# Decoder layer, feed-forward stage: tiles 8 to 15's reciprocals are split in three pieces by GpSimd instead of VectorE, and turned behind tile 7's first product

## The chip, the cores and the metric

The kernel runs on one core of a Trainium2 chip. The metric is the device time of one execution in microseconds (us); lower is better. Engines are called by their names: TensorE (PE in the profile, PEld for its weight loads), VectorE (DVE), ScalarE (ACT), GpSimd (POOL) and SyncE (SP), which issues the DMAs.

## What is computed

One post-norm decoder layer over 8 x 256 tokens of 512 numbers: self-attention with 16 heads, cross-attention, and a feed-forward part; after each the input is added and the sum normalised. Only the feed-forward part is touched. From the reference, cut:

```
def activation_quant(x):
    scale = 127.0 / jnp.clip(jnp.max(jnp.abs(x), axis=-1, keepdims=True), EPS, None)
    return jnp.clip(jnp.round(x * scale), -128.0, 127.0) / scale
def bitlinear(x, w, b):
    return jnp.einsum('bsd,fd->bsf', activation_quant(x), weight_quant(w)) + b
h = bitlinear(x, w1, b1)                # 512 -> 2048
h = jax.nn.gelu(h, approximate=False)
h = layernorm(h, gamma, beta)
return bitlinear(h, w2, b2)             # 2048 -> 512
```

weight_quant makes each weight -1, 0 or 1 times one factor. Each token row has a scale of its own in each of the two products.

## The kernel before

The 2048 tokens are 16 tiles of 128 rows, tile t = 0 to 15 (TILES). The feed-forward stage is a software pipeline over t in which each engine has a program of its own; engines meet only at semaphores, and each runs its own instructions in the order written. In round t of its loop (line numbers are those of the kernel before):

- TensorE: first product of tile t, `up(t, f)` for f = 0 to 3, each four matmuls with the weights (L1846) and one with the bias (L1847) into one of four PSUM banks; then the second product of tile t - 3, `down(t-3)`, one matmul L1864 and sixteen L1869. `up` waits for the gelu of the tile before to have emptied the banks, two banks at a time. Since the products are made with whole numbers, the bias must be divided by the row's factor: the reciprocal of that factor, split in three bf16 pieces (high, middle, low), stands as six rows for each token in `recips`, and L1847 multiplies them, turned into `rT`, with `bias_rows`.
- ScalarE: `gelu(t, 0)` and `gelu(t, 1)` (L2074, two banks each), `norm_y(t-4)` (L2115), `square(t)` (L2083), `round_h(t-1)` (L2094, to bytes), `spread_y(t-3)` (L2106, L2109).
- VectorE: `mean(t)` (L1969, one small instruction), `scale_gamma(t)` (L1979), `take_y(t-3)` (L2016), `norm_h(t)` (L1988), `scale_h(t)` (L1994, L1999, L2004).
- GpSimd: `bias_acc(t-2)` (L2154), `root_h(t)` (L2159, and L2164, a power), `round_x(t+3)` and `cut_x(t+3)` (L1932, L1939), `scale_out(t-1)` (L2169), `centre_y(t-3)` (L2180, a power L2185, and L2189).
- SyncE: turns `xq` into `xT` and `hq` into `hT` by DMA (L1793, L1803 to L1808) and stores the output.

What waits for what in a tile: `mean(t)` waits for both halves of gelu(t), square(t) for mean(t), root_h(t) for square(t), norm_h(t) for root_h(t), round_h(t) for scale_h(t), down(t) for the turned round_h(t), norm_y(t) for centre_y(t).

The reciprocals are made for eight tiles at a time. `scales(dve, 1)` (L1903 to L1927) does tiles 8 to 15 on VectorE in round 5 between take_y(2) and norm_h(5): nine instructions on 128x8 numbers. The first four make the scale of x (L1910, which round_x(8) on GpSimd waits for) and the reciprocal itself (L1913); the last five split it in three pieces. In round 7 TensorE turns the pieces for all eight tiles (`turn_recips`, two groups of four transposes, L1951) and ScalarE copies them from PSUM (`take_recips`, two copies L1956). The first product of tile 8 waits for the first of these copies, in this line of `up`:

```
if f == 0 and t % 4 == 0:
    pe.wait_ge(s["rT_ready"], t // 4 + 1)
```

Each copy waits for all eight transposes.

Of the kernel before, what the change touches and what calls it, by code (L numbers as in the profile page):

```python
# [12 lines left out]
ALU = mybir.AluOpType  # L13
# [3 lines left out]
P = 128  # L17
# [1682 lines left out]
def feed_forward(nc, T, out, env, keep):  # L1700
# [11 lines left out]
    with ExitStack() as ctx:  # L1712
# [3 lines left out]
        def sb(name, shape, dt=F32):  # L1716
# [29 lines left out]
        xg, xsc, xd, xr, hd, gsum, nm, ss, ve, rstd, hmax, hg, hs, ystats, ymv, yv, yr, ym, m_half, shift, ysum, ynm, yss = (  # L1746
            small[:, at:at + n] for at, n in zip(
                places, (16, 16, 16, 48, 16, 4, 2, 2, 2, 2, 2, 2, 2, 12, 4, 2, 2, 2, 1, 1, 2, 2, 2)))
        one = ones[:].bitcast(BF16)[:, 1:2]
        xr = xr.rearrange("p (c t) -> p c t", c=3)  # L1750
# [6 lines left out]
        s = {n: sem("f_" + n) for n in names}  # L1757
# [9 lines left out]
        def live(t):  # L1767
            return 0 <= t < TILES
# [63 lines left out]
        def tensor(pe):  # L1832
            def up(t, f):
                if f == 0:
                    pe.wait_ge(xT_in[t % 3], (t // 3 + 1) * 16)
                    if t == 0:
                        pe.wait_ge(w_in[0], 16)
                if f == 0 and t % 4 == 0:
                    pe.wait_ge(s["rT_ready"], t // 4 + 1)
                if t == 0:  # L1840
                    pe.wait_ge(env["shared_sems"]["rows_in"], 3 * 16)
                if f % 2 == 0 and t > 0:
                    pe.wait_ge(s["gelu_ready"], (t - 1) * 2 + f // 2 + 1)
                cols = slice(f * 512, (f + 1) * 512)
                for c in range(CH):
                    pe.matmul(psH[f], turned_x(t)[:, c, :], w1[:, c, cols], start=c == 0, stop=False)  # L1846
                pe.matmul(psH[f], rT[:, t, :], bias_rows[:, cols], start=False, stop=True).then_inc(s["f1"], 1)  # L1847

            def sum_w2():
                pe.wait_ge(w_in[1], 16)  # L1850
                pe.wait_ge(s["rT_ready"], 2)
                for k in range(FCH):
                    last = pe.matmul(psR[0:1, :], one, w2[:, k, :], start=k == 0, stop=k == FCH - 1)
                last.then_inc(s["w2_summed"], 1)

            def down(t):
                if t == 0:
                    pe.wait_ge(s["sums_ready"], 1)
                    pe.wait_ge(s["fconsts"], 33)
                if t > 1:  # L1860
                    pe.wait_ge(s["y_ready"], t - 1)
                else:
                    pe.wait_ge(env["shared_sems"]["y_out"], TILES - 1 + t)
                pe.matmul(psO[t % 2], less_base[:], w2_sums[:], start=True, stop=False)  # L1864
                pe.wait_ge(hT_in[t % 2], (t // 2 + 1) * 16)
                for k in range(FCH):
                    if t == TILES - 1 and k == HALF:
                        pe.wait_ge(last_in, 16)
                    last = pe.matmul(psO[t % 2], hT[:, t % 2, k, :], w2[:, k, :], start=False, stop=k == FCH - 1)  # L1869
                last.then_inc(s["f2"], 1)  # L1870

            tail = env["tail"]
            pe.wait_ge(env["shared_sems"]["clipped"], TILES * 4)
            for t in range(TILES + 3):
                if t == 7:
                    turn_recips(pe, 2)
                    turn_recips(pe, 3)
                for f in range(4):
                    if live(t):
                        up(t, f)  # L1880
                if t == 0:
                    tail["mix"]()
                if t == 1:
                    sum_w2()
                if t == 2:
                    tail["output"](0)
                    tail["output"](1)
                if live(t - 3):
                    down(t - 3)
# [13 lines left out]
        def scales(dve, g):  # L1903
            lo, hi = PARTS[g]
            now, n = slice(lo, hi), hi - lo
            dve.wait_ge(env["x_maxed"], hi)
            nc.vector.tensor_scalar(xg[:, now], xmax[:, now], EPS, 1.0 / QMAX, ALU.max, ALU.mult
                                    ).then_inc(s["x_guarded"], 1)
            dve.wait_ge(s["x_guarded"], 2 * g + 1)
            nc.vector.reciprocal(xsc[:, now], xg[:, now]).then_inc(s["x_scaled"], 1)  # L1910
            nc.vector.tensor_scalar(xd[:, now], xg[:, now], w_mean[:, 0:1], None, ALU.mult).then_inc(s["x_guarded"], 1)
            dve.wait_ge(s["x_guarded"], 2 * g + 2)
            nc.vector.reciprocal(xr[:, 0, now], xd[:, now]).then_inc(s["r_set"], 1)  # L1913
            dve.wait_ge(s["r_set"], 3 * g + 1)
            nc.vector.tensor_copy(recips[:, now, 0:3], xr[:, 0, now].unsqueeze(2).broadcast_to([P, n, 3])
                                  ).then_inc(s["r_split"], 1)
            dve.wait_ge(s["r_split"], 3 * g + 1)
            nc.vector.tensor_tensor(xr[:, 1, now], xr[:, 0, now], recips[:, now, 0], ALU.subtract
                                    ).then_inc(s["r_set"], 1)
            dve.wait_ge(s["r_set"], 3 * g + 2)  # L1920
            nc.vector.tensor_copy(recips[:, now, 3:5], xr[:, 1, now].unsqueeze(2).broadcast_to([P, n, 2])
                                  ).then_inc(s["r_split"], 1)
            dve.wait_ge(s["r_split"], 3 * g + 2)
            nc.vector.tensor_tensor(xr[:, 2, now], xr[:, 1, now], recips[:, now, 3], ALU.subtract
                                    ).then_inc(s["r_set"], 1)
            dve.wait_ge(s["r_set"], 3 * g + 3)
            nc.vector.tensor_copy(recips[:, now, 5], xr[:, 2, now]).then_inc(s["r_split"], 1)  # L1927

        def round_x(pool, t):
            if t in (lo for lo, _ in PARTS):  # L1930
# [23 lines left out]
        def take_recips(act, j):  # L1954
            act.wait_ge(s["r_turned"], j // 2 * 2 + 2)
            nc.scalar.copy(rT[:, 4 * j:4 * j + 4, :].rearrange("p t n -> p (t n)"),  # L1956
                           psR[:, (j % 2) * 256:(j % 2 + 1) * 256].bitcast(BF16)[0:6, :]
                           ).then_inc(s["rT_ready"], 1)
# [109 lines left out]
        def scalar(act):  # L2068
# [50 lines left out]
            for t in range(TILES + 4):  # L2119
                if live(t):  # L2120
                    gelu(t, 0)
                    gelu(t, 1)
                if t == 1:
                    tail["scale_y"](B - 2)
                    tail["late_norm"](B - 3)
                if t == 3:
                    tail["scale_y"](B - 1)
                    tail["late_norm"](B - 2)
                if t == 5:
                    tail["late_norm"](B - 1)  # L2130
                if t == 7:
                    take_recips(act, 2)
                    take_recips(act, 3)
                if live(t - 4) and t - 4 < TILES - 1:
                    norm_y(t - 4)
                if live(t):
                    square(t)
                if t == 0:
                    tail["round_o"]()
                if t == 2:  # L2140
                    take_sums()
                if live(t - 1):
                    round_h(t - 1)
                if live(t - 3) and t - 3 < TILES - 1:
                    spread_y(t - 3)

        def gpsimd(pool):
# [45 lines left out]
            for t in range(0, TILES + 3):  # L2193
                if live(t - 2):
                    bias_acc(t - 2)
                if live(t):
                    root_h(t)
                if t + 3 >= AHEAD and live(t + 3):
                    round_x(pool, t + 3)
                    cut_x(pool, t + 3)  # L2200
                if t == 0:
                    tail["split_o"]()
                    tail["root_sum"](B - 3)
                if t == 1:
                    pool.wait_ge(s["hn_ready"], 2)
                    tail["finish_ahead"](B - 2, 0)
                    tail["finish_ahead"](B - 2, 1)
                if t == 2:
                    tail["root_y"]()
                    tail["root_sum"](B - 2)  # L2210
                if t == 3:
                    pool.wait_ge(s["hn_ready"], 4)
                    tail["finish_ahead"](B - 1, 0)
                if t == 4:
                    tail["root_sum"](B - 1)
                if live(t - 1):
                    scale_out(t - 1)
                if live(t - 3):
                    centre_y(t - 3)
# [81 lines left out]
```

## Time and profile before

| | us |
|---|---|
| median of 3 runs | 1409.6 (1407.73 to 1410.35) |
| the profiled execution, its own time | 1409.61 |
| its span in the profile | 1407.8 |
| TensorE busy | 1373.2 (98%) |
| VectorE busy | 1180.7 (84%) |
| ScalarE busy | 798.8 (57%) |
| GpSimd busy | 646.4 (46%) |

Busy time is summed over all stages; the feed-forward stage takes about the last 170 us of the span. Times in the rows are microseconds from the span's start. In a timeline row the first number is the start, the second the duration; then come the engine, the line and the operation, and in brackets, where there is one, the idle time of the engine ahead of it and what ended it. The span is 1.8 us shorter than the execution's own time.

### The profile page before, as it was taken

The numbers are of one execution on the slowest core, as the hardware profiler recorded it, in microseconds if no ns is written. First come the engines' busy times: TensorE is split into PE (matmuls) and PEld (weight loads), VectorE is DVE, ScalarE is ACT, GpSimd is POOL, SyncE is SP. The second block draws the span as 40 slices with busy tenths as digits, with TensorE's granted clock in tenths as the row PEclk, the third lists the DMA queues.
The fourth block names the chain that finished last, engine by engine and source line by source line (L and its number), as shares of the span: only waits on it lengthen the run. The fifth ranks groups of instructions, "written<-read, shape, count | busy, mean of one in ns | idle before, by whom it ended". The sixth has DMA issues, their size and how long they took to land.

```text
span 1407.8 us, 25519 instructions
## 1 busy us (share of the span) xinstructions
PE 1373.2 (98%) x8642; PEld 1088.5 (77%) x8642; DVE 1180.7 (84%) x1966; ACT 798.8 (57%) x1856; POOL 646.4 (46%) x747
## 2 busy tenths in 40 slices
PE   8999999999999999999999999999999999898997
PEld 6888888888888888888888888887777777642332
DVE  6888888888879888888887888865778889899996
ACT  6444544545445454555555556754556555678895
POOL 6544435235333433433533444561344455656763
PEclk9999999999999999999999999999999999999998
DMA  7301101011010110102112111411000000522454
GB/s 284 121 11 37 62 14 45 30 46 35 28 58 15 45 60 1 31 28 71 53 46 76 60 38 48 147 46 46 17 16 16 16 15 13 193 69 53 101 106 104
DMA packets 73464, 81.00 MB, mean 58 GB/s; under 512 B 45960, under 2 KB 46472, under 8 KB 72846
## 3 DMA queue, kind: packets, MB, share of 16 engines
q1 hardware_dynamic: 73358, 79.78, 18.8%
q8 instruction: 43, 0.70, 0.2%
q14 instruction: 63, 0.52, 0.1%
HBM read 60.88 MB, written 8.40 MB: 49 GB/s over the span
## 4 chain that ended last, share of the span: by engine, by line
PE 79%; issue 7%; DVE 6%; POOL 5%; ACT 1%; DMA 1%; SPq 0%; POOLq 0%; DVEq 0%; ACTq 0%
PE psum L360 16%; PE psum L362 16%; PE psum L361 16%; PE psum L1111 4%; PE psum L425 4%; PE psum L404 4%; PE psum L1112 3%; PE psum L1113 3%; PE psum L413 3%; PE psum L1205 2%; PE psum L427 2%; PE psum L402 2%; PE psum L1217 1%; DVE xinv L1314 1%; PE psum L1222 1%
## 5 line engine op out<-in xcount | busy, mean ns | idle before, releaser
L866 POOL TENSOR_TENSOR qk<-rope_a,rope_b 128x512 f32<-128x512 f32 x128 | 177.1, 1383 | 496.1 <-DVE rope_b L591 496.1
L360 PE MATMUL psum<-x_hi,w_hi 128*128 128x512 f32 x512 | 209.9, 410 | 1.9 <-DVE x_lo L532 1.9
L362 PE MATMUL psum<-x_hi,w_lo 128*128 128x512 f32 x512 | 201.5, 394 | 0.0
L361 PE MATMUL psum<-x_lo,w_hi 128*128 128x512 f32 x512 | 200.7, 392 | 0.0
L591 DVE SCALAR_TENSOR_TENSOR rope_b<-psum,qk_bias,sin 64x512 f32<-64x512 f32 x256 | 191.9, 750 | 3.8
L715 ACT ACTIVATE e<-s 128x384 f32<-128x384 f32 x128 | 66.4, 518 | 208.1 <-DVE s L572 208.1
L360 PE MATMUL psum<-w_hi,x_hi 128*128 128x256 f32 x512 | 147.5, 288 | 1.2 <-DVE v L614 1.2
L362 PE MATMUL psum<-w_hi,x_lo 128*128 128x256 f32 x512 | 144.8, 283 | 0.0
L361 PE MATMUL psum<-w_lo,x_hi 128*128 128x256 f32 x512 | 144.7, 283 | 0.0
L729 ACT ACTIVATE e<-p 128x128 f32<-128x128 f32 x128 | 39.3, 307 | 175.8 <-DVE p L600 175.8
L634 DVE TENSOR_TENSOR acc<-psum,acc 128x512 f32<-128x512 f32 x128 | 88.5, 692 | 59.8 <-PE psum L362 44.0
L873 POOL TENSOR_TENSOR p<-p,inv 128x128 f32<-128x128 f32 (+1 forms) x256 | 121.7, 506 | 13.6 <-DVE inv L608 13.6
L600 DVE TENSOR_TENSOR p<-e,sgn 128x384 f32<-128x384 f32 x128 | 120.3, 979 | 1.8 <-ACT e L722 0.8
L1540 ACT ACTIVATE xe<-xe,mask_now 128x1024 f32<-128x1024 f32 x64 | 78.8, 1238 | 67.2 <-DVE xe L1307 67.2
L591 DVE SCALAR_TENSOR_TENSOR rope_a<-psum,qk_bias,cos 128x512 f32<-128x512 f32 x128 | 95.3, 744 | 24.8 <-PE psum L362 24.7
L362 PEld LDWEIGHTS psum<-x_hi,w_lo 128*128 128x128 f32 x512 | 96.8, 189 | 21.8
L360 PEld LDWEIGHTS psum<-x_hi,w_hi 128*128 128x128 f32 x512 | 97.2, 190 | 19.6 <-DVE w_lo L528 1.4
L361 PEld LDWEIGHTS psum<-x_lo,w_hi 128*128 128x128 f32 x512 | 97.2, 190 | 17.6
L360 PE MATMUL psum<-w_hi,z_hi 128*128 128x512 f32 x256 | 106.0, 414 | 0.0
L572 DVE SCALAR_TENSOR_TENSOR s<-psum,tri 128x384 f32<-128x384 f32 x128 | 70.7, 552 | 41.6 <-PE psum L404 41.6
L362 PE MATMUL psum<-w_hi,z_lo 128*128 128x512 f32 x256 | 100.4, 392 | 0.0
L361 PE MATMUL psum<-w_lo,z_hi 128*128 128x512 f32 x256 | 100.1, 391 | 0.0
(209 smaller groups left out, 3736.2 us busy)
## 6 DMA issues: line engine op xcount, KB each, us to landing
stage<-w_self_dram SPq DMA_DIRECT2D x64, 256.0 KB, 2.9
w_raw<-w_ffn_dram SPq DMA_DIRECT2D x32, 512.0 KB, 3.6
acc<-x_dram SPq DMA_DIRECT2D x4, 1024.0 KB, 6.0
w_signs<-w_sign SPq DMA_DIRECT2D x16, 256.0 KB, 2.1
xw_raw<-w_cross_dram SPq DMA_DIRECT2D x4, 1024.0 KB, 5.7
c_raw<-ctxT_dram SPq DMA_DIRECT2D x8, 512.0 KB, 3.5
w<-w_signs SPq DMA_DIRECT2D x2, 2048.0 KB, 12.1
out_dram<-yb SPq DMA_DIRECT2D x16, 256.0 KB, 2.3
```

Source lines behind the costliest of these rows:

```text
L360: pe.matmul(ps, ah, bh, start=n == 0, stop=False)
L361: pe.matmul(ps, ah, bl, start=False, stop=False)
L362: last = pe.matmul(ps, al, bh, start=False, stop=n == len(pairs) - 1)
L404: pe.matmul(psS[b][:, P:LW], q[:, b * S + P:(b + 1) * S], kk[:, b * S:(b + 1) * S], start=True, stop=True).then_inc(scores, 1)
L572: nc.vector.scalar_tensor_tensor(s[:, b, :], psS[b][:, 0:LW], SELF_SCALE, tri[:], ALU.mult, ALU.mult).then_inc(s_ready, 1)
L591: last = nc.vector.scalar_tensor_tensor(dst[o, which, :].rearrange("p (b s) -> p b s", b=2), ps[i, :].rearrange("p (b s) -> p b s", b=2), ...
L600: nc.vector.tensor_tensor(p[:, b, :], e[:, b, :], sgn[:, b, :], ALU.mult).then_inc(p_ready, 1)
L634: nc.vector.tensor_tensor(tile, o_bank(n + j)[:, :], tile, ALU.add).then_inc(o_added, 1)
L715: nc.scalar.activation(e[:, b, :], s[:, b, :], ACT.Abs)
L866: nc.gpsimd.tensor_tensor(qk[:, k % 2, which, :], rope_a[:, which, :], rope_b[:, which, :], ALU.add).then_inc(qk_ready, 1)
L873: last = nc.gpsimd.tensor_tensor(p[:, b, cols], p[:, b, cols], inv[:, b, rows:rows + 1].broadcast_to([P, n]), ALU.mult)
L1540: nc.scalar.activation(part, part, ACT.Exp, scale=mask_now[:, par, kt, 0:1], bias=mask_now[:, par, kt, 1:2]).then_inc(e_ready, 1)
```

## The change

Three places move. Of `scales`, the last five instructions become `split_recips`; for tiles 0 to 7 VectorE still runs them where it did, for tiles 8 to 15 GpSimd runs them in its round 5, behind cut_x(8) and ahead of scale_out(4). On TensorE the two turns of round 7 stand behind up(7) instead of ahead of it. On ScalarE the two copies of round 7 stand behind round_h(6) instead of ahead of norm_y(3).

```
@@ tensor
             for t in range(TILES + 3):
+                for f in range(4):
+                    if live(t):
+                        up(t, f)
                 if t == 7:
                     turn_recips(pe, 2)
                     turn_recips(pe, 3)
-                for f in range(4):
-                    if live(t):
-                        up(t, f)
@@ scales
             nc.vector.reciprocal(xr[:, 0, now], xd[:, now]).then_inc(s["r_set"], 1)
-            dve.wait_ge(s["r_set"], 3 * g + 1)
-            nc.vector.tensor_copy(recips[:, now, 0:3], xr[:, 0, now].unsqueeze(2).broadcast_to([P, n, 3])
-                                  ).then_inc(s["r_split"], 1)
...
-            dve.wait_ge(s["r_set"], 3 * g + 3)
-            nc.vector.tensor_copy(recips[:, now, 5], xr[:, 2, now]).then_inc(s["r_split"], 1)
+            if g == 0:
+                split_recips(dve, nc.vector, g)
+
+        def split_recips(eng, ops, g):
+            lo, hi = PARTS[g]
+            now, n = slice(lo, hi), hi - lo
+            eng.wait_ge(s["r_set"], 3 * g + 1)
+            ops.tensor_copy(recips[:, now, 0:3], xr[:, 0, now].unsqueeze(2).broadcast_to([P, n, 3])
+                            ).then_inc(s["r_split"], 1)
+            eng.wait_ge(s["r_split"], 3 * g + 1)
+            ops.tensor_tensor(xr[:, 1, now], xr[:, 0, now], recips[:, now, 0], ALU.subtract
+                              ).then_inc(s["r_set"], 1)
...
@@ scalar
-                if t == 7:
-                    take_recips(act, 2)
-                    take_recips(act, 3)
                 if live(t - 4) and t - 4 < TILES - 1:
                     norm_y(t - 4)
                 if live(t):
                     square(t)
...
                 if live(t - 1):
                     round_h(t - 1)
+                if t == 7:
+                    take_recips(act, 2)
+                    take_recips(act, 3)
                 if live(t - 3) and t - 3 < TILES - 1:
                     spread_y(t - 3)
@@ gpsimd
+                if t == 5:
+                    split_recips(pool, nc.gpsimd, 1)
                 if live(t - 1):
                     scale_out(t - 1)
```

What stands in a row on ScalarE in round 7, from gelu(7) to gelu(8), with the semaphores that an instruction waits for in brackets. Before:

```order
L2074 ACTIVATE h,fsmall<-psum,fsmall 128x1024 [waits f_u_ready,f_f1] x2
L1956 COPY rT<-psum 6x512 [waits f_r_turned] x2
L2115 ACTIVATE yb<-yb,fsmall 128x512 [waits f_y_centred]
L2083 ACTIVATE fspare,fsmall<-h,fsmall 128x2048 [waits f_vared,f_mean_ready]
L2094 ACTIVATE hq<-hn,fsmall 128x2048 [waits hT_in_0,f_h_scaled]
L2106 ACTIVATE fsmall<-fsmall 128x1 [waits f_y_centred,f_y_ready]
L2109 ACTIVATE fspare,fsmall<-yb,fsmall 128x512 [waits f_y_spread]
L2074 ACTIVATE h,fsmall<-psum,fsmall 128x1024 [waits f_u_ready,f_f1] x2
```

The same place on ScalarE in the changed kernel (its lines are numbered six higher):

```order
L2080 ACTIVATE h,fsmall<-psum,fsmall 128x1024 [waits f_u_ready,f_f1] x2
L2121 ACTIVATE yb<-yb,fsmall 128x512 [waits f_y_centred]
L2089 ACTIVATE fspare,fsmall<-h,fsmall 128x2048 [waits f_vared,f_mean_ready]
L2100 ACTIVATE hq<-hn,fsmall 128x2048 [waits hT_in_0,f_h_scaled]
L1962 COPY rT<-psum 6x512 [waits f_r_turned] x2
L2112 ACTIVATE fsmall<-fsmall 128x1 [waits f_y_centred,f_y_ready]
L2115 ACTIVATE fspare,fsmall<-yb,fsmall 128x512 [waits f_y_spread]
L2080 ACTIVATE h,fsmall<-psum,fsmall 128x1024 [waits f_u_ready,f_f1] x2
```

The two copies of `rT` moved back past norm_y(3), square(7) and round_h(6).

GpSimd in round 5 of the changed kernel, from root_h(5) to root_h(6); fsmall holds all the small per-row numbers:

```order
L2170 TENSOR_TENSOR fsmall<-fsmall 128x1 [waits f_hn_ready,f_vared]
L1938 TENSOR_SCALAR xs<-acc,fsmall 128x512 [waits f_x_scaled]
L1945 TENSOR_SCALAR xq<-xs 128x512 [waits xT_in_0,f_xs_ready]
L1921 CAST recips<-fsmall 128x8x3 [waits f_r_set]
L1924 TENSOR_TENSOR fsmall<-fsmall,recips 128x8 [waits f_r_split]
L1927 CAST recips<-fsmall 128x8x2 [waits f_r_set]
L1930 TENSOR_TENSOR fsmall<-fsmall,recips 128x8 [waits f_r_split]
L1933 CAST recips<-fsmall 128x8 [waits f_r_set]
L2175 TENSOR_TENSOR fsmall<-fsmall,w_mean 128x1 [waits f_h_guarded]
L2186 TENSOR_SCALAR fsmall<-fsmall 128x1 [waits f_y_spread]
L2191 TENSOR_TENSOR fsmall<-fsmall 128x1 [waits f_y_normed,f_y_guarded]
L2195 TENSOR_SCALAR fsmall<-fsmall 128x1 [waits f_y_rooted]
```

The five rows from L1921 to L1933 are new there; before, scale_out(4) (now L2175) followed cut_x(8) (now L1945) directly.

VectorE in round 5, the end of `scales` and what follows it, before:

```order
L1913 RECIPROCAL fsmall<-fsmall 128x8 [waits f_x_guarded]
L1915 CAST recips<-fsmall 128x8x3 [waits f_r_set]
L1918 TENSOR_TENSOR fsmall<-fsmall,recips 128x8 [waits f_r_split]
L1921 CAST recips<-fsmall 128x8x2 [waits f_r_set]
L1924 TENSOR_TENSOR fsmall<-fsmall,recips 128x8 [waits f_r_split]
L1927 CAST recips<-fsmall 128x8 [waits f_r_set]
L1988 SCALAR_TENSOR_TENSOR hn<-hn,fsmall,beta 128x2048 [waits f_u_ready,f_rooted]
```

In the changed kernel norm_h(5) follows L1913 directly.

## Rows read from the trace of the kernel before

**Rows 1.** Busy time by engine, granted clock (PEclk), from 1286 to 1394 us.

```profile
1286.00:1394.00 108.00, 99.28 (x406) 35.09 (x405) 104.77 (x114) 96.21 (x138) 68.91 (x104) 0.95 0.46 99
```

**Rows 2.** Timeline of VectorE, rounds 5 to 8 and tile 15's mean.

```profile
1298.63 0.20 DVE L1913 RECIPROCAL fsmall<-fsmall 128x8 f32<-128x8 f32 x1
...
1300.38 2.35 DVE L1988 SCALAR_TENSOR_TENSOR hn<-hn,fsmall,beta 128x2048 f32<-128x2048 f32 x1
...
1308.67 2.79 DVE L1988 SCALAR_TENSOR_TENSOR hn<-hn,fsmall,beta 128x2048 f32<-128x2048 f32 x1
...
1322.88 0.21 DVE L1969 TENSOR_SCALAR fsmall<-fsmall 128x1 f32<-128x1 f32 x1
1323.13 2.42 DVE L1979 SCALAR_TENSOR_TENSOR hn<-h,fsmall,gamma 128x2048 f32<-128x2048 f32 x1
...
1326.26 2.79 DVE L1988 SCALAR_TENSOR_TENSOR hn<-hn,fsmall,beta 128x2048 f32<-128x2048 f32 x1
...
1383.50 0.21 DVE L1969 TENSOR_SCALAR fsmall<-fsmall 128x1 f32<-128x1 f32 x1
```

**Rows 3.** Timeline of GpSimd, rounds 5 and 6.

```profile
1298.61 0.69 POOL L1932 TENSOR_SCALAR xs<-acc,fsmall 128x512 f32<-128x512 f32 x1 [1.32 <-DVE fsmall L1910]
...
1300.54 2.60 POOL L2185 TENSOR_TENSOR fsmall<-fsmall 128x1 f32<-128x1 f32 x1
...
1308.63 0.69 POOL L1932 TENSOR_SCALAR xs<-acc,fsmall 128x512 f32<-128x512 f32 x1
1309.40 2.53 POOL L1939 TENSOR_SCALAR xq<-xs 128x512 bf16<-128x512 f32 x1
...
1312.45 0.55 POOL L2185 TENSOR_TENSOR fsmall<-fsmall 128x1 f32<-128x1 f32 x1
1313.12 0.26 POOL L2189 TENSOR_SCALAR fsmall<-fsmall 128x1 f32<-128x1 f32 x1
```

**Rows 4.** Timeline of ScalarE, rounds 6 to 8.

```profile
1303.55 0.81 ACT L2115 ACTIVATE yb<-yb,fsmall 128x512 f32<-128x512 f32 x1 [2.07 <-POOL fsmall L2189]
1305.60 2.00 ACT L2083 ACTIVATE fspare<-h,fsmall 128x2048 f32<-128x2048 f32 x1 [1.24 <-DVE fsmall L1969]
...
1312.71 1.03 ACT L1956 COPY rT<-psum 6x512 bf16<-6x512 bf16 x2
...
1316.35 2.08 ACT L2094 ACTIVATE hq<-hn,fsmall 128x2048 uint8<-128x2048 f32 x1
...
1320.36 1.10 ACT L2074 ACTIVATE h<-psum,fsmall 128x1024 f32<-128x1024 f32 x1
```

**Rows 5.** Timeline of TensorE, rounds 5, 6, 8 and 9.

```profile
1278.05 1.02 PE L1846 MATMUL psum<-w,xT_ahead 128*128 128x512 bf16 x4 [2.07 <-ACT h L2074]
...
1290.51 1.27 PE L1846 MATMUL psum<-w,xT_ahead 128*128 128x512 bf16 x4 [3.48 <-ACT h L2074]
...
1298.41 0.38 PE L1847 MATMUL psum<-bias_rows,rT 6*128 6x512 bf16 x1
...
1313.37 1.02 PE L1846 MATMUL psum<-w,xT 128*128 128x512 bf16 x4 [1.33 <-ACT rT L1956]
...
1318.18 0.39 PE L1847 MATMUL psum<-bias_rows,rT 6*128 6x512 bf16 x1
...
1322.18 1.03 PE L1846 MATMUL psum<-w,xT 128*128 128x512 bf16 x4
```

**Rows 6.** Busy time and granted clock (0.50) inside the product at 1290.51.

```profile
1292.00:1294.00 2.00, 2.00 (x5) 0.43 (x4) 1.90 (x5) 1.97 (x4) 1.88 (x3) 0.50 0.71 138
```

**Rows 7.** Timeline of TensorE, the second products of tiles 14 and 15.

```profile
1392.19 5.97 PE L1869 MATMUL psum<-w,hT 128*128 128x512 bf16 x16 [3.91 <-DMA hT<-hq]
...
1398.41 3.63 PE L1869 MATMUL psum<-w,hT 128*128 128x512 bf16 x16
```

**Rows 8.** Timeline of SyncE's queue, issue of tile 15's first half.

```profile
1393.18 1.23 SPq L1805 DMA_TRANSPOSE hT<-hq  x1
```

**Rows 9.** The tile hT: its 17 transposing DMAs, from issue to landing.

```profile
DMA to landing us min/median/max: 3.1/4.3/4.9
```

More of the change, by code:

```diff
@@ L1913, in scales @@
             nc.vector.reciprocal(xr[:, 0, now], xd[:, now]).then_inc(s["r_set"], 1)
-            dve.wait_ge(s["r_set"], 3 * g + 1)
-            nc.vector.tensor_copy(recips[:, now, 0:3], xr[:, 0, now].unsqueeze(2).broadcast_to([P, n, 3])
-                                  ).then_inc(s["r_split"], 1)
[L1917 to L1925, printed above, removed]
-            dve.wait_ge(s["r_set"], 3 * g + 3)
-            nc.vector.tensor_copy(recips[:, now, 5], xr[:, 2, now]).then_inc(s["r_split"], 1)
+            if g == 0:
[9 more added lines that the diff above has]
+                              ).then_inc(s["r_set"], 1)
+            eng.wait_ge(s["r_set"], 3 * g + 2)
+            ops.tensor_copy(recips[:, now, 3:5], xr[:, 1, now].unsqueeze(2).broadcast_to([P, n, 2])
+                            ).then_inc(s["r_split"], 1)
+            eng.wait_ge(s["r_split"], 3 * g + 2)
+            ops.tensor_tensor(xr[:, 2, now], xr[:, 1, now], recips[:, now, 3], ALU.subtract
+                              ).then_inc(s["r_set"], 1)
+            eng.wait_ge(s["r_set"], 3 * g + 3)
+            ops.tensor_copy(recips[:, now, 5], xr[:, 2, now]).then_inc(s["r_split"], 1)
         def round_x(pool, t):
```

## The prediction

> **What bounds the kernel now.** I read the busy time of the stage first, then the timeline of each engine around the edit. From 1286 to 1394 us VectorE is busy 104.8 of 108 us [rows 1], so a reader's first thought is that work taken off it is time saved. But TensorE stands beside it as a second bound: from tile 8's first product to tile 9's it takes 8.81 us (1313.37 to 1322.18) [rows 5], and VectorE takes 8.80 us a tile (norm_h(6) at 1308.67, norm_h(8) at 1326.26, two tiles in 17.59) [rows 2]. What keeps the two apart is slack, not speed: up(8) ended at 1318.57 (1318.18 + 0.39) [rows 5], and mean(8), which needs its last gelu, ran at 1322.88 [rows 2]. From the end of a product to the mean behind it at least 1.27 us pass: a start of 0.04, the second gelu 1.10 with the read of its sum, about 1.19 together, and 0.04 [rows 4]. So TensorE is 1322.88 - 1318.57 - 1.27 = 3.04 us early at tile 8. What makes it later than that is paid, and since it can't run faster than 8.81 us a tile, it isn't won back.
>
> **Part one, the five instructions leave VectorE.** L1913 starts at 1298.63 and norm_h(5) at 1300.38 [rows 2]. Without the split norm_h(5) follows L1913 by some 0.08, at 1298.71, 1.67 us earlier. There it meets round_x(8) on GpSimd, 1298.61 to 1299.30 [rows 3]. One round later the same pair meets the same way: GpSimd's xs at 1308.63 for 0.69 (to 1309.32), norm_h(6) at 1308.67, which took 2.79 instead of 2.35 and ended at 1311.46, 2.14 behind xs's end [rows 2, 3]. So norm_h(5) ends at 1299.30 + 2.14 = 1301.44 instead of 1302.73: VectorE gains 1.29. mean(6) comes 2.63 behind norm_h's end (8.80 a tile, less 3.38 from mean to norm_h, less 2.79), at 1304.07, and scale_gamma(6) 0.25 later, at 1304.32 [rows 2].
>
> **Part two, the five instructions on GpSimd.** cut_x(8) now runs into norm_h(5), as cut_x(9) did into norm_h(6): from 1309.40 it took 2.53, to 1311.93, 0.47 behind norm_h's end [rows 2, 3]. So GpSimd comes to the split at 1301.44 + 0.47 = 1301.91. The trace has no such instruction on GpSimd. Nearest are its one-number operations: scale_out and the next one take 0.52 together (1311.93 to 1312.45) [rows 3], 0.26 each. These are 8 to 24 numbers wide, and each waits for the one before; I take 0.28, 1.40 us in all. The low end is VectorE's pace of 0.20 for such instructions, 1.0; the high end 0.69 each, what GpSimd takes for 512 numbers [rows 3], 3.4.
>
> Then come scale_out(4) and the start of centre_y(2), 0.52, its power at 1303.83, and 0.67 later (1312.45 to 1313.12) [rows 3] its multiply L2189, at 1304.50. That is 0.18 behind scale_gamma(6). And a small GpSimd instruction that starts while VectorE works on two inputs in SBUF is held to its end: the power at 1300.54 took 2.60 beside norm_h(5), against 0.55 at 1312.45 [rows 3]; it ended at 1303.14, 0.41 behind norm_h's 1302.73. scale_gamma(6) itself is held by the power (to 1304.38) and ends about 2.14 later, 1306.52; the multiply ends 0.13 behind it (0.41 less the 0.28 by which it is shorter), 1306.65.
>
> The Trainium skill speaks against the edit here (Perfetto Trace Analysis, Optimizing Scalar/DVE Operations: since GpSimd and VectorE share a read port of SBUF, moving work between those two might not help), and says which of them waits (SBUF — State Buffer, Who interferes with whom: whoever starts first keeps the port for the whole instruction). By that rule all hangs on 0.18 us of issue order; were the port shared in bandwidth, the multiply would end near 1304.8 and the sum would be that of the second rival below.
>
> norm_y(2) waits for this multiply already now (ScalarE idle 2.07, start 1303.55), and square(6) stands behind it in ScalarE's program [rows 4]. norm_y(2) now starts at 1306.68 and square(6) 0.8 later, 1307.5, instead of 1305.60: 1.9 late. norm_h(6) follows square(6) by 3.07 as before (1305.60 to 1308.67) [rows 2, 4], and round_h(6) is at 1316.35 + 1.9 = 1318.25 [rows 4]. VectorE's gain is gone.
>
> **Part three, the turn and the copies.** On TensorE the eight transposes swap places with up(7); they take the same in either place, the split is done by 1303.3, and down(4) ends where it did: 1313.37 - 1.33 = 1312.04 [rows 5]. up(8) waited 1.33 us for the first copy of rT, which started at 1312.71; product and copy are 0.66 apart [rows 4, 5]. Now the copies stand behind square(7) and round_h(6). round_h(6) takes 2.08 with 0.09 of overlap, so they start at 1318.25 + 1.99 = 1320.24, and up(8) at 1320.90: 7.5 us late, after 8.9 us of idle TensorE. What waits on ScalarE behind the copies, spread_y(4) and gelu(8), waits for up(8) anyway. Their old place gives nothing back: they ended at 1313.74 (1312.71 + 1.03) [rows 4], and square(7) had to wait for mean(7) at 1314.08 (1322.88 less 8.80) with only norm_y(3) between.
>
> **The clock.** up(6) started at 1290.51 after 3.48 us idle and ended at 1298.79, 8.28 us, where up(8) took 5.20 [rows 5]; inside it the granted clock was 0.50, the 1.2 GHz level [rows 6]. After 2.07 us idle four matmuls took 1.02, full speed [rows 5]. 8.9 us is past the longer of these, so I give up(8) 8.28 us: end 1329.18. The Trainium skill (TensorE: Matmul & The Clock Gate, The HAM clock gate) says that the engine returns to half clock when idle and that the number of slow matmuls at the start differs from run to run.
>
> **The sum.** mean(8) is at 1329.18 + 1.27 = 1330.45, 7.6 late. VectorE reaches mean(9) at 1339.25. TensorE starts up(9) 3.61 behind the end of up(8) as before (1318.57 to 1322.18) [rows 5], at 1332.79, and ends at 1337.99, which allows mean(9) at 1339.26: both engines now set the pace and TensorE is the slower. mean(15) = 1339.26 + 6 x 8.81 = 1392.1 instead of 1383.50 [rows 2]: 8.6 late. The end gives some of it back. Before, down(14) waited 3.91 us for its turned tile and then took 5.97 us at low clock, so down(15) started only at 1398.41, 3.63 long [rows 7], though its first half was issued at 1393.18 [rows 8] and landed 3.1 later [rows 9], at 1396.3. Now TensorE is 10.6 late (1322.18 to 1332.79) and the tile 8.6, so the wait is 3.91 - 2.0 = 1.9 us, under the 2.07 that left the clock up: down(14) takes 3.6 and down(15) starts when its half lands, 1396.3 + 8.6 = 1404.9, 6.5 later than before. After it nothing changes. 1409.61 + 6.5 = **1416.1**; the profiled execution stands at the median of 1409.6, so that needs no correction.
>
> **The rivals.**
> - *The long way* (0.21). The split takes over 1.9 us, the power itself meets scale_gamma(6) and waits too: 0.7 more, 1416.8. Or the clock falls before down(14) as well: 2.3 us more, 1418.4. Against the latter: 1.9 against 2.07.
> - *GpSimd slips through* (0.17). If the split takes under 1.2 us, the multiply starts ahead of scale_gamma(6), square(6) isn't late (about 0.2 early), and 2.1 us fall away: 1414.0. For it: only 0.18 us decide.
> - *The clock holds in up(8)* (0.10). 3.1 less: 1413.0. Against it: 0.50 after a shorter idle.
> - *The saving reaches the end* (0.05), not slower: VectorE's 1.29 us are carried through all later tiles, 1408.3. It decides at TensorE's slack of 3.04: up(8) would have to start before 1313.37 + 3.04 - 1.29 = 1315.1 at full clock. Against it: the copies can't start ahead of round_h(6)'s end, 1318.4 without any other delay; moving that up by all of 1.29 gives up(8) at 1317.7.
> - *Both small mercies* (0.03), GpSimd through and the clock up: 1409.61 + 6.5 - 2.1 - 3.1 = 1410.9, no change.
>
> **The numbers.** The forecast has 0.44. Within 0.2% (2.8 us, about what a measurement of this kernel can tell) lie the last two rivals, 0.08 less a little; faster needs more than VectorE can save at all, 0.01; slower 0.91. The range 1412.0 to 1419.0 leaves out the last two rivals, and of the long way the case in which both of its delays come together (1409.61 + 6.5 + 0.7 + 2.3 = 1419.1) or a third joins them; between them about 0.13.
>
> **What the profile after would show.** norm_h(5) at 1298.7 for about 2.8; five GpSimd instructions from 1301.9 for 1.4; centre_y(2)'s multiply held to about 1306.6; square(6) near 1307.5; TensorE idle some 9 us with the copy as its releaser, up(8) near 1320.9, 8.3 long at clock 0.5; mean(8) near 1330.4 with VectorE idle ahead of it; down(14) at full clock. Wrong would be: rT ready early, or TensorE running tiles in under 8.81 us once it is the late one, which would win the loss back.

## The result, and the profile after

| | us |
|---|---|
| before, median of 5 runs in the same job | 1409.57 (1407.73 to 1410.35) |
| changed kernel, median of 5 runs | 1417.14 (1415.96 to 1418.31) |
| ratio | 1.0056, 95% interval 1.0046 to 1.0067 |
| its profiled execution: own time, span | 1418.24, 1416.4 |

The change makes the kernel 7.6 us slower. The forecast was 1416.1 with a range of 1412.0 to 1419.0. The rows that answer to those of before follow; lines of the changed kernel are numbered six higher from L1915 on (norm_h is L1994, mean L1975, scale_gamma L1985). All times of this execution lie 1.29 us later than those of before already at L1913 (1299.92 against 1298.63 [rows 2]); where that comes from is told at the end, and the comparisons below are made from L1913 on.

Timeline of VectorE: start, duration, instruction, idle ahead and what ended it.

```profile
1299.92 0.20 DVE L1913 RECIPROCAL fsmall<-fsmall 128x8 f32<-128x8 f32 x1
1300.04 2.68 DVE L1994 SCALAR_TENSOR_TENSOR hn<-hn,fsmall,beta 128x2048 f32<-128x2048 f32 x1
...
1305.60 2.35 DVE L1985 SCALAR_TENSOR_TENSOR hn<-h,fsmall,gamma 128x2048 f32<-128x2048 f32 x1
...
1311.86 2.79 DVE L1994 SCALAR_TENSOR_TENSOR hn<-hn,fsmall,beta 128x2048 f32<-128x2048 f32 x1 [3.24 <-POOL fsmall L2170]
...
1331.62 0.21 DVE L1975 TENSOR_SCALAR fsmall<-fsmall 128x1 f32<-128x1 f32 x1 [5.47 <-ACT h L2080]
...
1340.63 0.21 DVE L1975 TENSOR_SCALAR fsmall<-fsmall 128x1 f32<-128x1 f32 x1
...
1393.36 0.21 DVE L1975 TENSOR_SCALAR fsmall<-fsmall 128x1 f32<-128x1 f32 x1 [0.16 <-ACT h L2080]
```

VectorE had no wait here before. Now it has two long ones: 3.24 us ahead of norm_h(6), and 5.47 us ahead of mean(8). What it saved shows in the first two rows: norm_h(5) 0.12 behind L1913 instead of 1.75.

Timeline of GpSimd, round 5 and the power of root_h(6).

```profile
1300.67 2.53 POOL L1945 TENSOR_SCALAR xq<-xs 128x512 bf16<-128x512 f32 x1
1303.15 0.21 POOL L1921 CAST recips<-fsmall 128x24 bf16<-128x24 f32 x1
...
1304.29 0.21 POOL L1933 CAST recips<-fsmall 128x8 bf16<-128x8 f32 x1
...
1304.99 0.55 POOL L2191 TENSOR_TENSOR fsmall<-fsmall 128x1 f32<-128x1 f32 x1
1305.66 2.42 POOL L2195 TENSOR_SCALAR fsmall<-fsmall 128x1 f32<-128x1 f32 x1
...
1311.28 0.55 POOL L2170 TENSOR_TENSOR fsmall<-fsmall 128x1 f32<-128x1 f32 x1
```

The five instructions take 0.21 each and follow each other by some 0.28, and nothing holds them. The multiply L2195 starts at 1305.66, 0.06 behind scale_gamma(6) at 1305.60, and takes 2.42 instead of 0.26 [rows 3]: it is held until scale_gamma(6) has ended (1307.95), and ends 0.13 behind it.

Timeline of ScalarE: norm_y(2), square(6), round_h(6), the two copies.

```profile
1308.11 0.81 ACT L2121 ACTIVATE yb<-yb,fsmall 128x512 f32<-128x512 f32 x1 [5.35 <-POOL fsmall L2195]
1308.84 1.99 ACT L2089 ACTIVATE fspare<-h,fsmall 128x2048 f32<-128x2048 f32 x1
...
1319.53 2.08 ACT L2100 ACTIVATE hq<-hn,fsmall 128x2048 uint8<-128x2048 f32 x1
1321.51 1.04 ACT L1962 COPY rT<-psum 6x512 bf16<-6x512 bf16 x2
```

Timeline of TensorE: up(8) from its first to its last matmul, up(9), down(14), down(15).

```profile
1322.17 1.87 PE L1846 MATMUL psum<-w,xT 128*128 128x512 bf16 x4 [9.69 <-ACT rT L1962]
...
1329.96 0.38 PE L1847 MATMUL psum<-bias_rows,rT 6*128 6x512 bf16 x1
...
1333.96 1.03 PE L1846 MATMUL psum<-w,xT 128*128 128x512 bf16 x4
...
1402.35 3.63 PE L1869 MATMUL psum<-w,hT 128*128 128x512 bf16 x16 [2.29 <-DMA hT<-hq]
...
1407.07 3.63 PE L1869 MATMUL psum<-w,hT 128*128 128x512 bf16 x15 [0.78 <-DMA hT<-hq]
```

Busy time and granted clock inside up(8).

```profile
1324.00:1326.00 2.00, 2.00 (x6) 0.49 (x5) 1.93 (x3) 0.00 (x0) 1.72 (x5) 0.50 0.32 66
```

TensorE waits 9.69 us for the first copy (1.33 before [rows 5]), and up(8) then takes 8.17 us, 1322.17 to 1330.34, for the most part at a granted clock of 0.50, the 1.2 GHz level (the last four of its weight matmuls take 1.04 again, full speed). At the end down(14) waits 2.29 us instead of 3.91, and takes 3.63 instead of 5.97 [rows 7].

### The profile page after: what moved, and what is told of

The parts are those of the page before. It is cut to its first block, busy times and chain, and to the rows that moved or that the text cites. A ratio compares the mean times of both kernels' runs of the same rounds, so it can differ in the third digit from the quotient of the medians.

```text
span 1416.4 us, 25505 instructions
## 1 busy us (share of the span) xinstructions
PE 1373.0 (97%) x8628; PEld 1088.6 (77%) x8642; DVE 1180.5 (83%) x1961; ACT 798.7 (56%) x1856; POOL 649.5 (46%) x752
## 4 chain that ended last, share of the span: by engine, by line
PE 79%; issue 7%; DVE 6%; POOL 6%; ACT 1%; DMA 1%; SPq 0%; POOLq 0%; DVEq 0%; ACTq 0%
PE psum L360 16%; PE psum L362 16%; PE psum L361 16%; PE psum L1111 4%; PE psum L425 4%; PE psum L404 4%; PE psum L1112 3%; PE psum L1113 3%; PE psum L413 3%; PE psum L1205 2%; PE psum L427 2%; PE psum L402 2%; PE psum L1217 2%; PE psum L1222 1%; DVE xinv L1314 1%
```

## The experiments

Eight kernels. Each took its ratio against the kernel before, run beside it on the same chip; x1 to x4 ran in one job (before 1409.42, 29 runs), x5 to x8 in another (before 1409.16, 23 runs). The last column is from the one profiled execution of each: the time from L1913 to the end of the span, less the 109.17 us (1407.8 - 1298.63) of before. The changed kernel has +7.3 there.

| kernel | median, us | ratio | 95% interval | from L1913 on, us |
|---|---|---|---|---|
| x1_turn_copies | 1414.32 | 1.0036 | 1.0023 to 1.0049 | +8.8 |
| x2_copies_early | 1412.84 | 1.0020 | 1.0011 to 1.0029 | +1.0 |
| x3_split_behind | 1409.62 | 1.0001 | 0.9993 to 1.0010 | +0.4 |
| x4_square_first | 1410.46 | 1.0007 | 0.9998 to 1.0015 | -0.5 |
| x5_filler | 1413.34 | 1.0033 | 1.0020 to 1.0046 | +5.1 |
| x6_no_split | 1407.47 | 0.9994 | 0.9986 to 1.0003 | -1.8 |
| x7_copies_mid | 1412.86 | 1.0032 | 1.0020 to 1.0044 | +4.0 |
| x8_fill_tail | 1407.17 | 0.9989 | 0.9981 to 0.9998 | -2.0 |

The two measures needn't agree. A single execution carries whatever TensorE's clock did in it, and the ratio carries what lies ahead of the edit too: in these executions L1913 stands anywhere from 1295.56 to 1302.13. So each cause below is read from the trace, as a distance from L1913, and the ratio says only whether it shows in the time.

### x1_turn_copies: the turn and the copies alone

```
-            if g == 0:
-                split_recips(dve, nc.vector, g)
+            split_recips(dve, nc.vector, g)
...
-                if t == 5:
-                    split_recips(pool, nc.gpsimd, 1)
```

> The split stays on VectorE as in the kernel before; only the turn (behind up(7)) and the two copies (behind round_h(6)) are moved. Theory (the late copies starve TensorE): up(8) starts 5.6 us late against the other engines, after some 7 us of idle TensorE, takes 8.2 us at half clock, mean(15) is 6.6 us late, and the time is 4.5 to 5.3 us above before, 1414 to 1415. Rival (the loss comes from GpSimd's held multiply): within 0.5 us of before, 1409.6.

Measured 1.0036, 5.1 us of 1409.4. Timeline of TensorE, up(8):

```profile
1318.43 1.86 PE L1846 MATMUL psum<-w,xT 128*128 128x512 bf16 x4 [8.82 <-ACT rT L1961]
```

L1913 stands at 1298.09 in this execution, so up(8) starts 20.34 behind it, against 14.74 before (1298.63 to 1313.37 [rows 2, 5]): 5.6 late, as the theory has it. By the ratios this half of the change costs about two thirds of the loss, and it has nothing on the other side: no work is saved by it.

Two parts of the expectation missed in this execution. up(8) took 9.46 us, not 8.2, and the low clock went on through down(5):

```profile
1328.25 6.02 PE L1869 MATMUL psum<-w,hT 128*128 128x512 bf16 x16
```

So mean(15) is 10.5 us late, not 6.6. The execution took 1417.89, the slowest of five with a median of 1414.32, so how late mean(15) is in the median run isn't known.

### x2_copies_early: the split on GpSimd alone

The changed kernel with the two copies back ahead of norm_y(3):

```
+                if t == 7:
+                    take_recips(act, 2)
+                    take_recips(act, 3)
                 if live(t - 4) and t - 4 < TILES - 1:
                     norm_y(t - 4)
```

> As the changed kernel, split on GpSimd and turn behind up(7), but the copies of rT in their old place ahead of norm_y(3). Theory: the multiply of centre_y(2) is held, norm_h(6) is 1.9 us late, up(8) waits about as before (1.3 us) and runs at full clock: 1.9 us above before, 1411.5. Rival (without the late copies VectorE's saving reaches the end): 1408.3.

Measured 1.0020, 2.8 us (1.6 to 4.1). With x1 the ratios add up to the whole change, 0.0036 + 0.0020 = 0.0056, which with these intervals is good to about 2 us; the last column doesn't add up (8.8 and 1.0 against 7.3), mostly for x1's clock. Timeline of GpSimd, the multiply:

```profile
1307.84 2.37 POOL L2195 TENSOR_SCALAR fsmall<-fsmall 128x1 f32<-128x1 f32 x1
```

Timeline of VectorE: L1913, norm_h(6), mean(8).

```profile
1302.13 0.20 DVE L1913 RECIPROCAL fsmall<-fsmall 128x8 f32<-128x8 f32 x1
...
1313.99 2.79 DVE L1994 SCALAR_TENSOR_TENSOR hn<-hn,fsmall,beta 128x2048 f32<-128x2048 f32 x1 [3.16 <-POOL fsmall L2170]
...
1328.19 0.21 DVE L1975 TENSOR_SCALAR fsmall<-fsmall 128x1 f32<-128x1 f32 x1
```

Timeline of TensorE, up(8):

```profile
1318.71 1.87 PE L1846 MATMUL psum<-w,xT 128*128 128x512 bf16 x4 [3.19 <-ACT rT L1962]
```

norm_h(6) comes 11.86 behind L1913, 1.82 later than before (10.04). One part of the expectation was wrong: up(8) doesn't wait 1.3 us at full clock but 3.19, and starts at half clock (four matmuls in 1.87). The copies are late with square(6) while TensorE isn't, which the expectation left out. up(8) takes 6.76 us. mean(8) nevertheless stands 26.06 behind L1913, 1.81 more than before (24.25), no more than norm_h(6): TensorE's slack of 3.04 took the rest. At the end 1.0 us is left, since down(14) took 5.08 instead of 5.97.

### x3_split_behind: the same split, four instructions later

```
-                if t == 5:
-                    split_recips(pool, nc.gpsimd, 1)
                 if live(t - 1):
                     scale_out(t - 1)
                 if live(t - 3):
                     centre_y(t - 3)
+                if t == 5:
+                    split_recips(pool, nc.gpsimd, 1)
```

> As x2_copies_early, but GpSimd does the split behind centre_y(2), at the end of its round 5. Theory (what costs is that centre_y(2), which norm_y(2) and square(6) wait for, stands behind the split): the multiply takes 0.26 and ends near 1303.4, square(6) starts 1.2 us earlier than before, the fifth instruction of the split is held by scale_gamma(6) instead, root_h(6) follows late, norm_h(6) 0.2 us later than before: 1409.8. Rival (the split costs 1.4 us on GpSimd wherever it stands): 1411.5.

Measured 1.0001. Timeline of GpSimd: the multiply, the split's fifth instruction.

```profile
1301.66 0.27 POOL L2195 TENSOR_SCALAR fsmall<-fsmall 128x1 f32<-128x1 f32 x1
...
1303.01 2.29 POOL L1933 CAST recips<-fsmall 128x8 bf16<-128x8 f32 x1
```

Timeline of VectorE: L1913, norm_h(6).

```profile
1297.20 0.20 DVE L1913 RECIPROCAL fsmall<-fsmall 128x8 f32<-128x8 f32 x1
...
1307.45 2.79 DVE L1994 SCALAR_TENSOR_TENSOR hn<-hn,fsmall,beta 128x2048 f32<-128x2048 f32 x1 [1.55 <-POOL fsmall L2170]
```

Now the fifth instruction is held, 2.29 for 0.21, and bias_acc(4) and root_h(6) behind it. norm_h(6) is 10.25 behind L1913, 0.21 more than before, where 0.2 was expected. The five instructions cost GpSimd the same time as in x2_copies_early, so it isn't their length alone that costs 1.8 us but who stands behind them. The turn stands behind up(7) here as in the changed kernel, so its place costs nothing that this run shows; what x1_turn_copies pays for is the copies.

### x4_square_first: ScalarE doesn't wait for the multiply

```
-                if live(t - 4) and t - 4 < TILES - 1:
+                if live(t - 4) and t - 4 < TILES - 1 and t != 6:
                     norm_y(t - 4)
                 if live(t):
                     square(t)
+                if t == 6:
+                    norm_y(t - 4)
```

> As x2_copies_early, but ScalarE does square(6) ahead of norm_y(2) in round 6, so that square(6) doesn't wait for GpSimd's multiply. Theory: the multiply is still held to the end of scale_gamma(6), square(6) starts right behind mean(6), 1.3 us earlier than before, but bias_acc(4) and root_h(6) stand behind the multiply on GpSimd, so that norm_h(6) comes out some 0.1 us later than before: 1409.7. Rival (the chain through ScalarE isn't what carries the 1.9 us): the same time as x2_copies_early.

Measured 1.0007 (0.9998 to 1.0015), which includes 1, no change; its median is below x2_copies_early's, though the two intervals overlap. Timelines of GpSimd and VectorE: the held multiply, norm_h(6).

```profile
1307.18 2.42 POOL L2197 TENSOR_SCALAR fsmall<-fsmall 128x1 f32<-128x1 f32 x1
...
1311.78 2.79 DVE L1994 SCALAR_TENSOR_TENSOR hn<-hn,fsmall,beta 128x2048 f32<-128x2048 f32 x1 [1.64 <-POOL fsmall L2172]
```

L1913 stood at 1301.44, so norm_h(6) is 10.34 behind it, 0.30 over before (0.1 was expected) instead of 1.82. The multiply is held as in x2; that it no longer stands ahead of square(6) takes 1.5 us away. That shows the way of the loss: GpSimd's multiply, norm_y(2), square(6).

### x5_filler: TensorE kept busy while it waits

```
+        FILL = 40
...
                 if live(t - 3):
                     down(t - 3)
+                if t == 7:
+                    for k in range(FILL):
+                        pe.matmul(bank[4], xT_ahead[:, 0, k % CH, :], w1[:, k % CH, 0:512], start=k == 0, stop=k == FILL - 1)
```

> The changed kernel, with 40 matmuls of 512 columns on TensorE between down(4) and up(8), into a PSUM bank that nobody reads, so that TensorE isn't idle while it waits for the copies of rT. They take 8.6 us and end about 1 us before the first copy. Theory (the idle time costs a second time, through the clock): up(8) starts as late as in the changed kernel but takes 5.2 us instead of 8.2, mean(8) and all behind it are 3 us earlier, 1414 if the changed kernel is at 1417. Rival (the clock doesn't carry any of the loss, or the fillers delay up(8)): the changed kernel's time or more.

Measured 1.0033 against the changed kernel's 1.0056 (in another job, each by its own runs of before): 3.2 us less, give or take some 2.4. Timeline of TensorE: the fillers, first and last matmul of up(8).

```profile
1310.54 8.80 PE L1893 MATMUL psum<-w,xT_ahead 128*128 128x512 bf16 x39
1320.33 1.02 PE L1847 MATMUL psum<-w,xT 128*128 128x512 bf16 x4 [0.99 <-issue]
...
1325.15 0.39 PE L1848 MATMUL psum<-bias_rows,rT 6*128 6x512 bf16 x1
```

up(8) starts 22.17 behind L1913 (1298.16), as late as in the changed kernel (22.25), and takes 5.21 us instead of 8.17: the clock was worth 3.0 us there, and mean(15) is 3.05 earlier. At the end 2.2 of it is left (5.1 against 7.3 in the last column), because down(14) met the low clock in this execution:

```profile
1397.50 5.31 PE L1870 MATMUL psum<-w,hT 128*128 128x512 bf16 x16 [2.26 <-DMA hT<-hq]
```

### x6_no_split: what could be had at all

```
-            pe.wait_ge(s["r_split"], 3 * part_of(4 * j) + 3)
+            pe.wait_ge(s["r_split"], 3)
...
-                last = pe.transpose(ps[0:6, i * P:(i + 1) * P], recips[:, 4 * j + i, :], ident_b[:])
+                last = pe.transpose(ps[0:6, i * P:(i + 1) * P], recips[:, 4 * (j % 2) + i, :], ident_b[:])
```

with the copies as in x2 and no call of split_recips for tiles 8 to 15.

> No split for tiles 8 to 15 on any engine: the pieces of tiles 0 to 7 are turned a second time in their place (so the bias of tiles 8 to 15 is scaled wrongly), turn behind up(7), copies in their old place. It bounds what taking the five instructions off VectorE can be worth. Theory: norm_h(5) meets round_x(8) and is held 0.3 to 0.4 us, norm_h(6) is 1.3 us earlier than before against L1913, 1408.3. Rival (a full 1.7 us, or nothing because another engine is the bound): 1407.9 or 1409.6.

Measured 0.9994 (0.9986 to 1.0003): 0.8 us by the ratio, not told from nothing, and not from the 1.3 expected. Timeline of VectorE: L1913, norm_h(5), norm_h(6).

```profile
1299.64 0.20 DVE L1913 RECIPROCAL fsmall<-fsmall 128x8 f32<-128x8 f32 x1
1299.76 2.68 DVE L1994 SCALAR_TENSOR_TENSOR hn<-hn,fsmall,beta 128x2048 f32<-128x2048 f32 x1
...
1308.45 2.79 DVE L1994 SCALAR_TENSOR_TENSOR hn<-hn,fsmall,beta 128x2048 f32<-128x2048 f32 x1
```

The trace is sharper than the runs' times: norm_h(6) is 8.81 behind L1913, 1.23 earlier than before, and mean(15) is still 1.10 earlier. (The span gains 1.8, since down(14) took 5.31 instead of 5.97.) So what taking these five instructions off VectorE can give is about 1.2 us, 0.09%: it does reach the end, but is too small for this kernel's runs to show.

### x7_copies_mid: the copies 2 us earlier

As x1_turn_copies, with the copies between square(7) and round_h(6):

```
                 if live(t):
                     square(t)
+                if t == 7:
+                    take_recips(act, 2)
+                    take_recips(act, 3)
                 if t == 0:
                     tail["round_o"]()
```

> As x1_turn_copies (split on VectorE, turn behind up(7)), but the two copies stand between square(7) and round_h(6) instead of behind round_h(6), 2 us earlier. Theory (the loss follows the copies' place, less TensorE's slack): up(8) starts 3.6 us late instead of 5.6, after some 7 us idle at half clock, and the time is 2 us below x1_turn_copies, 1412 to 1413. Rival (a copy behind square(7) costs the same wherever it stands): x1_turn_copies' time.

Timeline of TensorE, up(8):

```profile
1320.34 1.87 PE L1846 MATMUL psum<-w,xT 128*128 128x512 bf16 x4 [4.94 <-ACT rT L1961]
```

L1913 stood at 1301.98: up(8) is 18.36 behind it, 2.0 earlier than in x1_turn_copies and 3.6 later than before, as expected. The idle time ahead of it was 4.94 where some 7 was expected, and the low clock still came: up(8) took 9.13. The time, 1.0032 against 1.0036 with intervals that overlap, doesn't tell the two apart; the medians differ by 1.5 us in the expected sense. As a measurement of time this run is inconclusive.

### x8_fill_tail: the give-back at the end

The kernel before, with 16 such matmuls ahead of down(14):

```
+        FILL = 16
...
+                if t == TILES + 1:
+                    for k in range(FILL):
+                        pe.matmul(bank[4], xT_ahead[:, 0, k % CH, :], w1[:, k % CH, 0:512], start=k == 0, stop=k == FILL - 1)
                 if live(t - 3):
                     down(t - 3)
```

> The kernel before, with 16 matmuls of 512 columns on TensorE ahead of down(14), into a PSUM bank that nobody reads; they take 3.5 of the 3.9 us in which TensorE waits for the turned tile. Theory (the idle time there lowers the clock, which the prediction reckoned as given back when the wait grew short): down(14) takes 3.6 us instead of 5.97, down(15) then waits for its own turned half, and the end comes 1.4 to 2.1 us earlier, 1407.5 to 1408.2. Rival (the fillers don't hold the clock, or the end is set by the turned half anyway): 1409.6.

Measured 0.9989 (0.9981 to 0.9998), 1.5 us faster than before by the ratio; the lowest median here, not told from x6_no_split's. Timeline of TensorE: the fillers, down(14), down(15).

```profile
1384.72 3.62 PE L1891 MATMUL psum<-w,xT_ahead 128*128 128x512 bf16 x16
...
1389.37 3.40 PE L1870 MATMUL psum<-w,hT 128*128 128x512 bf16 x15 [0.71 <-DMA hT<-hq]
...
1393.37 3.63 PE L1870 MATMUL psum<-w,hT 128*128 128x512 bf16 x16 [0.28 <-DMA hT<-hq]
```

down(14) runs at full clock and down(15) waits for its own half; the end is 2.0 us earlier against L1913. That is the mechanism by which the prediction gave back 2.1 us of the delay.

## Why the prediction was right

Distances from L1913, which take out the 1.29 us that the two executions differ by ahead of the edit:

| step | predicted | after |
|---|---|---|
| norm_h(5) ends | 2.81 | 2.80 |
| the split, from its start to scale_out(4) | 1.40 | 1.28 |
| the multiply starts behind scale_gamma(6) | 0.18 | 0.06 |
| norm_h(6) later than before | 1.9 | 1.90 |
| TensorE idle ahead of up(8) | 8.9 | 9.69 |
| up(8) starts | 22.27 | 22.25 |
| up(8) takes | 8.28 | 8.17 |
| mean(8) | 31.82 | 31.70 |
| mean(9) | 40.63 | 40.71 |
| mean(15) later than before | 8.6 | 8.57 |
| given back at the end | 2.1 | 1.2 |

- **VectorE's saving.** 1.67 us less 0.38 for the meeting with round_x(8) was reckoned; norm_h(5) ended 2.80 behind L1913 where it had ended 4.10 behind it [rows 2], 1.30 saved, and x6_no_split shows 1.23 at norm_h(6).
- **GpSimd.** The multiply took 2.42, 2.37 and 2.42 us in the changed kernel, x2 and x4, the split's fifth instruction 2.29 in x3, and 0.21 to 0.27 each where scale_gamma wasn't running. These rows agree with the Trainium skill's rule (SBUF — State Buffer, Who interferes with whom) that the first to start keeps the port. It was closer than reckoned, 0.06 us instead of 0.18: the five instructions took 1.28 where 1.40 had been an estimate from other instructions. Some 0.07 less still would have let GpSimd slip through, so that the estimate fell on the right side was luck. That the kernel itself falls there isn't: the multiply is 0.03 to 0.06 behind scale_gamma(6) in all four traces with this order (the changed kernel, x2, x4, x5).
- **The copies.** They cost 5.6 us of start, shown alone by x1_turn_copies and at a second place by x7_copies_mid. TensorE was idle 9.69 us and not 8.9 because down(4) had ended 0.85 earlier; up(8) starts by the copy, so this changed nothing.
- **The clock.** 3.0 us of up(8)'s length, shown by x5_filler. The prediction's 8.28 came from another tile; the same place took 9.46 in x1 and 9.13 in x7, so 8.17 is one outcome of several.
- **TensorE can't catch up.** From up(9) at 1333.96 to up(15) at 1386.88 it took 8.82 us a tile, though it was the late engine (ScalarE idle 0.91 us ahead of the second gelu in each round from 9 on). mean(8) was 7.45 late and mean(15) 8.57: nothing was won back.
- **The give-back** is the term that was mis-sized: 1.2 us instead of 2.1. That down(14) would run at full clock behind a wait of 1.9 us was right (2.29 us, 3.63 long). But down(15)'s half landed 3.75 us after its issue (1403.32 to 1407.07) where the least of the 17 landings, 3.1 [rows 9], had been taken, and in the last tiles norm_y, which before was done ahead of mean(t), now stands between the late gelu and square(t), which puts norm_h(15) 3.60 behind mean(15) instead of 3.32. Together 0.9. That the clock stayed up is in part luck. The prediction had set 1.9 us against the 2.07 that left it up, but the wait was 2.29, and 2.26 us at the same place in x5_filler were followed by 5.31; down(15) started 5.57 behind down(14) there and 4.72 here, so the low clock would have put the end some 0.85 us later.

The forecast of 1416.1 was 1.0 us under the median, of which this makes 0.9; that the sum comes so near is also chance, since the five runs themselves lie 2.4 us apart. The profiled execution itself was 1.29 us slow for a cause of its own.

## What to carry to other kernels

Before work is taken off a busy engine, look for a second one that keeps the same pace: here it left 3 us of slack, so that 1.2 us of saved work could bring 1.2 us at most, while a consumer that was put 5.6 us later used up the slack and cost the rest. An instruction in an in-order queue is priced by who stands behind it: the same five cost 1.8 us ahead of a value that ScalarE's queue waits for, and 0.2 us behind it. A wait of TensorE can cost twice, if its clock falls: 9.7 us idle brought 3.0 us more.

## What the runs showed of the hardware

- **A clock dip in unchanged code moves whole runs by over a microsecond.** The 1.29 us between the two profiled executions arise in cross-attention, some 80 us ahead of the edit, where the two kernels run the same instructions. Busy time and granted clock there, before:

```profile
1216.00:1218.00 2.00, 1.63 (x33) 0.93 (x26) 2.00 (x3) 1.36 (x2) 1.97 (x2) 1.00 0.70 167
```

and in the changed kernel:

```profile
1216.00:1218.00 2.00, 2.00 (x28) 1.30 (x20) 1.79 (x2) 1.31 (x2) 1.96 (x2) 0.52 0.64 155
```

In both, TensorE had stood idle 1.41 and 0.93 us in the 4 us ahead, between groups of small matmuls. By 1228 us the two executions are 1.23 us apart. That such dips also spread the runs of one kernel over some 2 us is a guess; no run tested it.

- **The clock after an idle time isn't the same at every time.** After 2.29 us down(14) ran in 3.63 us in the changed kernel; in x2_copies_early it took 5.08 after 2.44:

```profile
1397.61 5.08 PE L1869 MATMUL psum<-w,hT 128*128 128x512 bf16 x16 [2.44 <-DMA hT<-hq]
```

In x5_filler 2.26 us were followed by 5.31, and the fall came inside down(14): the granted clock was 0.90 in its first microsecond (1397.50 to 1398.50) and 0.50 behind it. Nor is 2.07 us safe: before, the four matmuls behind it took 1.02 [rows 5], in x3_split_behind, at the same place after the same 2.07, they took 1.86 at 0.50:

```profile
1276.61 1.86 PE L1846 MATMUL psum<-w,xT_ahead 128*128 128x512 bf16 x4 [2.07 <-ACT h L2080]
```

So the length of the idle time just ahead doesn't by itself say whether the clock falls. In x1_turn_copies the low clock outlasted up(8) and lasted through most of down(5), in the changed kernel it ended within up(8).
